# One place among 512 slots for every edge of a graph convolution: one comparison per column, the overflow counts three steps later, the list's chunks two per three steps

## The chip, the cores and the metric

The kernel runs on one core of one Trainium2 chip. The time is that of one execution on the device, in microseconds (us); several runs are given by their median. A core has a TensorE (PE in the profile) for matrix products, a VectorE (DVE), a ScalarE (ACT), a GpSimd (POOL) and a SyncE (SP) that issues transfers. Each works through its own list in order, and they wait for each other by semaphores.

## What is computed

Two relational graph convolutions, a residual and a layer norm, over 1250 nodes of 768 features, 21250 edges and 8 relations:

```python
def _rgcn_conv(x, src, dst, etype, W, root, b):
    x_src = x[src]
    seg = dst * num_rel + etype
    sums = jax.ops.segment_sum(x_src, seg, num_segments=num_nodes * num_rel)
    cnt = jax.ops.segment_sum(jnp.ones((src.shape[0],), dtype=x.dtype), seg, num_segments=num_nodes * num_rel)
    mean = sums / jnp.maximum(cnt, 1.0)[:, None]
    mean = mean.reshape(num_nodes, num_rel, -1)
    out = jnp.einsum('nri,rio->no', mean, W)
    return out + x @ root + b
...
h = jax.nn.relu(_rgcn_conv(x, src, dst, edge_type, W1, root1, b1))
out = _rgcn_conv(h, src, dst, edge_type, W2, root2, b2)
x = _layernorm(x + out)
```

## The kernel before

**The products.** The nodes lie in T = 10 tiles of 125 rows. For one relation the kernel multiplies all node tiles with the relation's weights, in STEPS = 20 steps: a step is one node tile by one half (384) of the output columns. A step is 18 matmuls of 128x384 on PE (L722), because each fp32 product is made of three, high by high, high by low and low by high. ScalarE stages the result (L624), SyncE stores it to `y`. Weights come in half units: a transfer into `w_raw`, ScalarE's `w_high` (L578, released by the steps with s = 1 and s = 11 of each relation), then `w_low`, a subtraction that the GpSimd makes for units 1 to 8 (L463) and the DVE for the others. This text counts steps through the relations: relation 2's s = 1 is step 41, relation 3's s = 11 is step 71. Steps 0 to 79 are the first four relations; the product with root1 (`matrix(ROOT1, ...)`) follows.

**The list of edges.** Rows of `y` are later gathered edge by edge and summed by destination. For that the kernel first sorts the edges into slots: for each pair of relation and destination tile (80 keys) 2 blocks of 128 slots, and further blocks for overflows. While PE multiplies, the DVE works out, for the 21250 edges held as 125 partitions by 170 columns, the key, the rank of an edge within its key (`ranks`, L1166 and L1171), and the rank among the overflows (L1179 to L1196). Both rankings need counts summed over the partitions, which is a small matmul of PE: `sum_rows` (L758) before step 16, and `sum_overs` (L764) before step 41, which waits for the DVE's L1186.

Then the list itself is made by matmuls with one-hot matrices, in CHUNKS = 17 chunks of CJ = 10 columns. For a chunk the DVE makes `key_hot` (L1207), `slot_hot` (L1215), `dst_hot` (L1217) and `keyed` (L1220, L1224). `slot_hot` compares, for each of the ten columns, 512 slots: the first 256 with `rank`, the other 256 with `rank2`, in two instructions. PE's `table_chunk` (L863, L867) multiplies them, 50 small matmuls a chunk, and adds all chunks up in PSUM. The buffers are double: the DVE may begin chunk c when PE has counted chunk c - 2 (`chunk_counted`), and PE waits for chunk c by `hot_ready`.

**The order around the change.** It is written out by hand: `chunks_at(step)` says which chunks PE takes behind a step, one behind every second step from TABLE_AT = 46 on, the last behind step 78. When all are counted, the DVE reads the sums (from L1249 on) and makes the indices by which the GpSimd gathers rows of `y` (L476); the first gathered rows are summed (L749) from the root product's step s = 10 on. PE's `sum_flags` stands behind the root product's s = 1.

Of the kernel before, what the change touches and what calls it, by code (L numbers as in the profile page):

```python
# [8 lines left out]
def rgcn_residual_layernorm(nc, x, src, dst, etype, w_all, b1, b2, out):  # L9
# [18 lines left out]
    N, D = x.shape  # L28
# [3 lines left out]
    P = 128  # L32
    K = D // P
    HALF = D // 2
    T = -(-N // P)
# [11 lines left out]
    MEAN_EDGES = NT * E / N / R  # L47
    FULL = int(MEAN_EDGES // P)
    OVER = 2
    OVER_CAPACITY = OVER * P - P // 2  # L50
    BLOCKS = FULL + OVER
    assert FULL == 2 and R == 8
    DIV_SHIFT = 17
# [16 lines left out]
    CJ = 10  # L70
    CHUNKS = EJ // CJ
    ROOT1 = R // 2
    TABLE_AT = 2 * STEPS + 6
    assert N < 2048 and TABLE_AT + 2 * CHUNKS - 1 <= ROOT1 * STEPS
    MEAN1 = R
    ROOT2 = R + 2
    MEAN2 = Q - 1
# [5 lines left out]
    with ctx:  # L83
# [198 lines left out]

        def chunks_at(step):
            n = step - TABLE_AT
            return [n // 2] if n >= 0 and n % 2 == 0 and n // 2 < CHUNKS else []

        def one_relation(g, r):
            return lambda s: [("sum", g, r, t) for t in range(T) if s == 3 + (STEPS - 4) * t // (T - 1)]
# [37 lines left out]
        def banks(shift, turning=False):  # L326
            return lambda s: 2 + s % 2 if turning and s >= T else (s + shift) % BANKS
# [103 lines left out]
        def _(pool):  # L431
# [11 lines left out]
            pool.memset(eps[:], EPS)  # L443
            pool.iota(column_i[:], [[1, P]], base=0, channel_multiplier=0)
            pool.iota(row_base_i[:].rearrange("p (r t) -> p r t", t=T), [[N, R], [0, T]], base=0, channel_multiplier=0)
            pool.iota(slot_i[:, 0:FULL * P], [[1, FULL * P]], base=0, channel_multiplier=0)
            pool.iota(slot_i[:, FULL * P:SLOTS - P // 2], [[1, OVER_CAPACITY]], base=0, channel_multiplier=0)
            pool.iota(slot_i[:, SLOTS - P // 2:SLOTS], [[1, P // 2]], base=P, channel_multiplier=0)
            link(pool.memset(identity[:], 0.0))
            pool.affine_select(out=identity[:], in_=identity[:], compare_op=ALU.not_equal, fill=1.0, base=0,  # L450
                               pattern=[[-1, P]], channel_multiplier=1)
# [257 lines left out]
        def _(pe):  # L709
# [127 lines left out]
            def staged(yc, turning=False):  # L837

                def free(s):
                    if isinstance(yc, int) and yc == 0 and s < BANKS:  # L840
                        return []
                    return [(y_staged, STEPS * yc + s + 1 - (2 if turning and s >= T else BANKS))]
                return free
# [54 lines left out]
            matrix(0, banks(0), lambda s: staged(0)(s) + ([(h_low_ready, 2 * s + 2)] if s < T else []), turning_x,  # L898
                   middle=(STEPS - 4, sum_rows))
            matrix(1, banks(0), staged(1))  # L900
            matrix(2, banks(0), staged(2), middle=(1, sum_overs), after=table_chunks(2))
            matrix(3, banks(0), staged(3), after=table_chunks(3))

            for s in range(STEPS):
# [27 lines left out]
        def _(dve):  # L932
# [182 lines left out]
            for t in range(4):  # L1115
# [2 lines left out]
            turns_after = iter((1, 2) * T)  # L1118


            tile, dl, src_f, key, row, gid, flag, rank, spos, rank2, src_up, dl_up, etype_f = \
                [edge_f[:, n, :] for n in range(13)]
            ups = edge_f[:, 10:13, :]
            INT = [edge_i[:, n, :] for n in range(4)]
# [68 lines left out]
                ins = dve.scalar_tensor_tensor(ranks[:, c, :], ranks[:, c, :], small[0:EP, 2, c:c + 1],  # L1193
                                               is_over[:, c, :], ALU.add, ALU.mult)
            link(ins)
            sum_ranks(rank2, T)  # L1196
            link(dve.tensor_scalar(flag, flag, -1.0, 1.0, ALU.mult, ALU.add))
            link(dve.scalar_tensor_tensor(spos, rank, float(P - FULL * P), flag, ALU.add, ALU.mult))
            link(dve.tensor_tensor(rank2, rank2, spos, ALU.add))


            dve.wait_ge(transposed, 2 * T)
            for c in range(CHUNKS):
                if c >= 2:
                    dve.wait_ge(chunk_counted, c - 1)
                cut = slice(c * CJ, (c + 1) * CJ)
                ins = dve.tensor_tensor(key_hot[:, c % 2], small_bf[0:EP, 0, :].unsqueeze(1).to_broadcast([EP, CJ, NB]),  # L1207
                                        key_bf[:, cut].unsqueeze(2).to_broadcast([EP, CJ, NB]), ALU.is_equal)
                ins.then_inc(dve_step, 1)
                steps[0] += 1  # L1210
                made = steps[0]
                for j in range(CJ):
                    e = c * CJ + j
                    for part, of in ((slice(0, FULL * P), rank), (slice(FULL * P, SLOTS), rank2)):
                        dve.tensor_scalar(slot_hot[:, c % 2, j, part], slot[0:EP, part], of[:, e:e + 1], None,  # L1215
                                          ALU.is_equal)
                dve.tensor_tensor(dst_hot[:, c % 2], column[0:EP, :].unsqueeze(1).to_broadcast([EP, CJ, P]),  # L1217
                                  dl_bf[:, cut].unsqueeze(2).to_broadcast([EP, CJ, P]), ALU.is_equal)
                values = ups[:, :, cut].rearrange("p n j -> p j n").unsqueeze(2)
                dve.tensor_tensor(keyed[:, c % 2, :, 0:3 * T].rearrange("p j (t n) -> p j t n", n=3),  # L1220
                                  is_over[:, :, cut].rearrange("p t j -> p j t").unsqueeze(3)
                                  .to_broadcast([EP, CJ, T, 3]), values.to_broadcast([EP, CJ, T, 3]), ALU.mult)
                dve.wait_ge(dve_step, made)
                dve.tensor_tensor(keyed[:, c % 2, :, 3 * T:KEYED].rearrange("p j (k n) -> p j k n", n=2),  # L1224
                                  key_hot[:, c % 2].unsqueeze(3).to_broadcast([EP, CJ, NB, 2]),
                                  values[:, :, :, 0:2].to_broadcast([EP, CJ, NB, 2]), ALU.mult)\
                    .then_inc(hot_ready, 1)
# [1 line left out]

            dve.scalar_tensor_tensor(row, etype_f, float(N), src_f, ALU.mult, ALU.add)  # L1230
            dve.scalar_tensor_tensor(gid, key, float(P), dl, ALU.mult, ALU.add)
            link(dve.tensor_scalar(flag, rank2, float(OVER_CAPACITY), None, ALU.is_ge))
            dve.tensor_copy(payload[:, :, 0], row)
            dve.tensor_copy(payload[:, :, 1], gid)
            link(dve.tensor_tensor_scan(spos, flag, flag, 0.0, ALU.add, ALU.max))
# [147 lines left out]
```

## Time and profile before

| | us |
|---|---|
| median of 3 runs | 1595.92 (1595.27 to 1596.81) |
| the profiled execution | 1587.02 |
| its span | 1585.2 |
| PE busy | 1480.5 (93% of the span) |
| DVE busy | 1047.0 (66%) |
| POOL busy | 617.9 (39%) |
| ACT busy | 573.1 (36%) |

The span is the time between the first and the last instruction of the program in the profile. Busy time is the time in which an engine had an instruction under way. PE overlaps its matmuls, so that each row of one is longer than the distance to the next; the DVE's instructions overlap a little too when none waits for the one before it. The granted clock is the share of TensorE's full clock that it was given.

### The profile page before, as it was taken

The numbers are of one execution on the slowest core, as the hardware profiler recorded it, in microseconds if no ns is written. First come the engines' busy times: TensorE is split into PE (matmuls) and PEld (weight loads), VectorE is DVE, ScalarE is ACT, GpSimd is POOL, SyncE is SP. The second block draws the span as 40 slices with busy tenths as digits, with TensorE's granted clock in tenths as the row PEclk, the third lists the DMA queues.
The fourth block names the chain that finished last, engine by engine and source line by source line (L and its number), as shares of the span: only waits on it lengthen the run. The fifth ranks groups of instructions, "written<-read, shape, count | busy, mean of one in ns | idle before, by whom it ended". The sixth has DMA issues, their size and how long they took to land.

```text
span 1585.2 us, 23968 instructions
## 1 busy us (share of the span) xinstructions
PE 1480.5 (93%) x9014; PEld 1458.6 (92%) x9014; DVE 1047.0 (66%) x1767; ACT 573.1 (36%) x818; POOL 617.9 (39%) x456
## 2 busy tenths in 40 slices
PE   5999799999999997998989799999999999899995
PEld 5999689989999997998989799999999999899895
DVE  6899999984877675786971022545454545488697
ACT  3222111111344453485552110333333333358442
POOL 1121111121678784664720320424343434366461
PEclk9999899999999998999999899999999999999998
DMA  5353131232667775775523441646465556577443
GB/s 162 114 187 124 38 99 45 75 97 91 208 210 216 240 243 186 219 223 178 142 83 131 146 158 40 194 154 208 158 200 174 189 177 191 171 235 208 120 143 125
DMA packets 102647, 249.80 MB, mean 158 GB/s; under 512 B 12607, under 2 KB 75758, under 8 KB 102486
## 3 DMA queue, kind: packets, MB, share of 16 engines
q0 software_dynamic: 31680, 131.81, 27.4%
q1 hardware_dynamic: 70870, 116.69, 22.2%
q8 instruction: 62, 1.02, 0.2%
q14 instruction: 35, 0.29, 0.0%
HBM read 204.47 MB, written 65.49 MB: 170 GB/s over the span
## 4 chain that ended last, share of the span: by engine, by line
PE 55%; DVE 22%; DMA 13%; issue 3%; POOL 3%; ACT 2%; SPq 0%; POOLq 0%; DVEq 0%; ACTq 0%
PE prod L722 43%; PE agg L749 11%; DMA raw<-y,bucket_index 6%; DMA y<-y_stage 5%; DVE slot_hot L1215 5%; POOL raw L476 2%; DVE ranks L1171 2%; DVE ranks L1166 2%; DMA x_rows<-in_x 2%; DVE keyed L1224 2%; DVE g_low L988 2%; DVE dst_hot L1217 1%; DVE ranks L1158 1%; DVE g_low L991 1%; PE prod L713 1%
## 5 line engine op out<-in xcount | busy, mean ns | idle before, releaser
L722 PE MATMUL prod<-w_high,h_high 128*128 128x384 f32 x2160 | 735.0, 340 | 20.4 <-ACT y_stage L624 13.3
L722 PE MATMUL prod<-w_low,h_high 128*128 128x384 f32 x2160 | 728.3, 337 | 0.0
L722 PE MATMUL prod<-w_high,h_low 128*128 128x384 f32 x2160 | 727.8, 337 | 0.0
L476 POOL DMA_INDIRECT raw<-y,bucket_index x380 | 494.2, 1301 | 542.3 <-DVE g_low L991 279.3
L991 DVE TENSOR_TENSOR g_low<-raw,g_high 128x768 fp32r<-128x768 f32 x280 | 259.6, 957 | 300.5 <-ACT g_high L591 298.9
L722 PEld LDWEIGHTS prod<-w_high,h_high 128*128 128x128 f32 x2160 | 410.9, 190 | 23.0 <-ACT y_stage L624 15.9
L722 PEld LDWEIGHTS prod<-w_low,h_high 128*128 128x128 f32 x2160 | 410.7, 190 | 0.0
L722 PEld LDWEIGHTS prod<-w_high,h_low 128*128 128x128 f32 x2160 | 409.8, 190 | 0.0
L624 ACT ACTIVATE y_stage<-prod 128x384 f32<-128x384 f32 x280 | 137.5, 492 | 723.5 <-PE prod L722 654.8
L591 ACT ACTIVATE g_high<-raw 128x768 fp32r<-128x768 f32 x300 | 243.2, 842 | 98.1 <-DMA raw<-y,bucket_index 78.5
L749 PE MATMUL agg<-g_high,one_hot 128*128 128x384 f32 x760 | 201.8, 347 | 22.5 <-DVE g_low L991 19.9
L749 PE MATMUL agg<-g_low,one_hot 128*128 128x384 f32 x680 | 175.6, 339 | 0.0
L749 PEld LDWEIGHTS agg<-g_high,one_hot 128*128 128x128 f32 x760 | 135.6, 189 | 33.1 <-issue 21.7
L463 POOL TENSOR_TENSOR w_low<-w_raw,w_high 128x2304 fp32r<-128x2304 f32 x8 | 47.3, 5911 | 266.0 <-ACT w_high L578 266.0
L749 PEld LDWEIGHTS agg<-g_low,one_hot 128*128 128x128 f32 x680 | 125.6, 190 | 0.0
L1001 DVE SCALAR_TENSOR_TENSOR acc<-agg,inv_count,acc 128x768 f32<-128x768 f32 x120 | 121.5, 1012 | 6.0 <-PE agg L749 5.8
L947 DVE TENSOR_TENSOR w_low<-w_raw,w_high 128x2304 fp32r<-128x2304 f32 (+1 forms) x37 | 72.8, 1967 | 56.5 <-ACT w_high L578 56.5
L578 ACT ACTIVATE w_high<-w_raw 128x2304 fp32r<-128x2304 f32 x36 | 76.5, 2126 | 58.0 <-PE prod L722 41.4
L588 ACT ACTIVATE g_high<-raw,scale 128x768 fp32r<-128x768 f32 x80 | 71.2, 932 | 69.7 <-DMA raw<-y,bucket_index 34.5
L980 DVE TENSOR_SCALAR one_hot<-column,dst_local 128x128 fp32r<-128x128 bf16 x380 | 89.6, 295 | 6.9 <-issue 6.4
L969 DVE TENSOR_TENSOR acc<-prod,acc 128x384 f32<-128x384 f32 x60 | 33.1, 555 | 79.6 <-PE prod L722 79.0
L1215 DVE TENSOR_SCALAR slot_hot<-slot,edge_f 125x256 f16<-125x256 f16 x340 | 82.9, 330 | 0.0
(137 smaller groups left out, 777.8 us busy)
## 6 DMA issues: line engine op xcount, KB each, us to landing
y<-y_stage SPq DMA_DIRECT2D x280, 187.5 KB
w_raw<-in_w_all SPq DMA_DIRECT2D x36, 1152.0 KB, 8.7
raw<-y,bucket_index POOLq DMA_INDIRECT x380, 5.3
x_rows<-in_x SPq DMA_DIRECT2D x10, 375.0 KB
y<-in_x SPq DMA_DIRECT2D x1, 3750.0 KB, 14.9
y<-acc SPq DMA_DIRECT2D x10, 375.0 KB
acc<-in_x SPq DMA_DIRECT2D x10, 375.0 KB
out<-acc SPq DMA_DIRECT2D x10, 375.0 KB
```

The source lines that it names most:

```text
L476: pool.indirect_dma_start(raw[:, i % NRAW, :], None, y[0:written * N, :], bass.IndirectOffsetOnAxis(ap=bucket_index[:, at_column:at_column ...
L578: act.activation(w_high[:, h], w_raw[:], ACT.Copy).then_inc(w_high_ready, 1)
L588: act.activation(g_high[:, split_slot(g, i), :], raw[:, slot, :], ACT.Copy, scale=scale[:, i:i + 1])\
L591: act.activation(g_high[:, split_slot(g, i), :], raw[:, slot, :], ACT.Copy).then_inc(high_ready, 1)
L624: act.activation(y_stage[:, s % BANKS, :], prod[:, bank, 0:HALF], ACT.Copy)\
L722: mm = pe.matmul(prod[:, bank, 0:HALF], left[:, k, t * P:(t + 1) * P], right[:, h, k, :], start=(k == 0 and left is h_high and right is w_ ...
L749: mm = pe.matmul(agg[:, par, c, 0:HALF], one_hot[:, par, b, :], part[:, split_slot(g, i), c * HALF:(c + 1) * HALF], start=(b == 0 and part ...
L947: ins = dve.tensor_tensor(w_low[:, h, part], w_raw[:, part], w_high[:, h, part].bitcast(f32), ALU.subtract)
L980: ins = dve.tensor_scalar(one_hot[:, par, b, :], column[:], dst_local[:, bass.ds(column_of(r, t, b), 1)], None, ALU.is_equal)
L991: ins = dve.tensor_tensor(low[p:P, split_slot(g, i), :], rows, high, ALU.subtract)
L1001: ins = dve.scalar_tensor_tensor(a, agg[:, t % 2, :, 0:HALF], inv_count[:, bass.ds(r * T + t, 1)], a, ALU.mult, ALU.add)
L1215: dve.tensor_scalar(slot_hot[:, c % 2, j, part], slot[0:EP, part], of[:, e:e + 1], None, ALU.is_equal)
```

## The change

- The DVE works out one number for each edge, `place`, among all 512 slots: the rank where it is below 256, 256 plus the overflow rank for an overflow, and for relation 0, whose third block is half of the last one, the rank plus 128. `slot` holds 0 to 447 and then 384 to 447. So `slot_hot` is one comparison of 512 columns for each edge column. Ahead of the chunks this takes five small operations in place of three.
- PE's `sum_overs` stands before relation 2's s = 4 (step 44) in place of s = 1 (step 41).
- `chunks_at` gives two chunks per three steps: behind steps 51, 52, 54, 55, 57, 58, ... and the last behind step 75.

```diff
-    TABLE_AT = 2 * STEPS + 6
-    assert N < 2048 and TABLE_AT + 2 * CHUNKS - 1 <= ROOT1 * STEPS
+    TABLE_AT = 2 * STEPS + 10
+    assert N < 2048 and TABLE_AT + CHUNKS * 3 // 2 + 1 <= ROOT1 * STEPS
...
         def chunks_at(step):
             n = step - TABLE_AT
-            return [n // 2] if n >= 0 and n % 2 == 0 and n // 2 < CHUNKS else []
+            return range(n * 2 // 3, min((n + 1) * 2 // 3, CHUNKS)) if n >= 0 else range(0)
...
-            pool.iota(slot_i[:, 0:FULL * P], [[1, FULL * P]], base=0, channel_multiplier=0)
-            pool.iota(slot_i[:, FULL * P:SLOTS - P // 2], [[1, OVER_CAPACITY]], base=0, channel_multiplier=0)
-            pool.iota(slot_i[:, SLOTS - P // 2:SLOTS], [[1, P // 2]], base=P, channel_multiplier=0)
+            pool.iota(slot_i[:, 0:SLOTS - P // 2], [[1, SLOTS - P // 2]], base=0, channel_multiplier=0)
+            pool.iota(slot_i[:, SLOTS - P // 2:SLOTS], [[1, P // 2]], base=SLOTS - P, channel_multiplier=0)
...
-            matrix(2, banks(0), staged(2), middle=(1, sum_overs), after=table_chunks(2))
+            matrix(2, banks(0), staged(2), middle=(4, sum_overs), after=table_chunks(2))
...
-            sum_ranks(rank2, T)
-            link(dve.tensor_scalar(flag, flag, -1.0, 1.0, ALU.mult, ALU.add))
-            link(dve.scalar_tensor_tensor(spos, rank, float(P - FULL * P), flag, ALU.add, ALU.mult))
-            link(dve.tensor_tensor(rank2, rank2, spos, ALU.add))
+            sum_ranks(place, T)
+            dve.tensor_scalar(gid, spos, -1.0, 1.0, ALU.mult, ALU.add)
+            link(dve.scalar_tensor_tensor(row, rank, float(FULL * P), spos, ALU.is_ge, ALU.add))
+            link(dve.tensor_tensor(gid, gid, rank, ALU.mult))
+            link(dve.scalar_tensor_tensor(gid, row, float(P), gid, ALU.mult, ALU.add))
+            link(dve.tensor_tensor(place, place, gid, ALU.add))
...
-                    for part, of in ((slice(0, FULL * P), rank), (slice(FULL * P, SLOTS), rank2)):
-                        dve.tensor_scalar(slot_hot[:, c % 2, j, part], slot[0:EP, part], of[:, e:e + 1], None,
-                                          ALU.is_equal)
+                    dve.tensor_scalar(slot_hot[:, c % 2, j, :], slot[0:EP, :], place[:, e:e + 1], None, ALU.is_equal)
...
-            link(dve.tensor_scalar(flag, rank2, float(OVER_CAPACITY), None, ALU.is_ge))
+            link(dve.tensor_scalar(flag, place, float(SLOTS - P // 2), None, ALU.is_ge))
```

The lines of the changed kernel stand two lower from the DVE's part on, so that L1215 becomes L1214 and L764 becomes L762.

The DVE's instructions ahead of the first chunk and in it, before:

```order
L1161 TENSOR_TENSOR edge_f<-ranks 125x170 [waits dve_step]
L1197 TENSOR_SCALAR edge_f<-edge_f 125x170 [waits dve_step]
L1198 SCALAR_TENSOR_TENSOR edge_f<-edge_f 125x170 [waits dve_step]
L1199 TENSOR_TENSOR edge_f<-edge_f 125x170 [waits dve_step]
L1207 TENSOR_TENSOR key_hot<-small_bf,key_bf 125x800 [waits transposed,dve_step]
L1215 TENSOR_SCALAR slot_hot<-slot,edge_f 125x256 x20
L1217 TENSOR_TENSOR dst_hot<-column,dl_bf 125x1280
L1220 TENSOR_TENSOR keyed<-is_key,edge_f 125x10x30
L1224 TENSOR_TENSOR keyed<-key_hot,edge_f 125x10x160 [waits dve_step]
```

The same place of the changed kernel:

```order
L1159 TENSOR_TENSOR edge_f<-ranks 125x170 [waits dve_step]
L1195 TENSOR_SCALAR edge_f<-edge_f 125x170 [waits dve_step]
L1196 SCALAR_TENSOR_TENSOR edge_f<-edge_f 125x170
L1197 TENSOR_TENSOR edge_f<-edge_f 125x170 [waits dve_step]
L1198 SCALAR_TENSOR_TENSOR edge_f<-edge_f 125x170 [waits dve_step]
L1199 TENSOR_TENSOR edge_f<-edge_f 125x170 [waits dve_step]
L1207 TENSOR_TENSOR key_hot<-small_bf,key_bf 125x800 [waits transposed,dve_step]
L1214 TENSOR_SCALAR slot_hot<-slot,edge_f 125x512 x10
L1215 TENSOR_TENSOR dst_hot<-column,dl_bf 125x1280
L1218 TENSOR_TENSOR keyed<-is_key,edge_f 125x10x30
L1222 TENSOR_TENSOR keyed<-key_hot,edge_f 125x10x160 [waits dve_step]
```

Twenty comparisons of 256 columns have become ten of 512, and two operations of 170 columns have come in ahead of key_hot.

PE from step 50 on, before. Each row that waits for `y_staged` is the first matmul of a step, the seventeen others are left out; each that waits for `hot_ready` is the first of a chunk:

```order
L722 MATMUL prod<-w_high,h_high 128x384 [waits y_staged,w_low_ready,w_high_ready]
...
L863 MATMUL agg<-keyed_60,slot_hot_59 128x160 [waits hot_ready]
...
L722 MATMUL prod<-w_high,h_high 128x384 [waits y_staged]
...
L722 MATMUL prod<-w_high,h_high 128x384 [waits y_staged]
...
L863 MATMUL agg<-keyed_60,slot_hot_59 128x160 [waits hot_ready]
...
L722 MATMUL prod<-w_high,h_high 128x384 [waits y_staged]
```

PE from step 50 on in the changed kernel:

```order
L720 MATMUL prod<-w_high,h_high 128x384 [waits y_staged,w_low_ready,w_high_ready]
...
L720 MATMUL prod<-w_high,h_high 128x384 [waits y_staged]
...
L861 MATMUL agg<-keyed_60,slot_hot_59 128x160 [waits hot_ready]
...
L720 MATMUL prod<-w_high,h_high 128x384 [waits y_staged]
...
L861 MATMUL agg<-keyed_60,slot_hot_59 128x160 [waits hot_ready]
...
L720 MATMUL prod<-w_high,h_high 128x384 [waits y_staged]
```

Chunk 2 stood behind step 50 and chunk 3 behind step 52; now chunk 0 stands behind step 51 and chunk 1 behind step 52.

## Rows read from the trace of the kernel before

**Rows 1.** Waits of PE, whole span: us in total, times, longest us
```profile
PE agg L749 <- DVE g_low L991: 19.9, 10, 8.0
...
PE prod L722 <- ACT y_stage L624: 13.3, 4, 10.0
PE agg L863 <- DVE keyed L1224: 10.7, 4, 3.7
PE agg L764 <- DVE small_bf L1186: 9.6, 1, 9.6
```

**Rows 2.** Chain of work that ended last: start us, us, what
```profile
56.43 24.99 PE prod L722 x144
```

**Rows 3.** Timeline of PE, steps 40 to 79: start, us, instruction [idle before <-releaser]
```profile
159.21 0.34 PE L722 MATMUL prod<-w_high,h_low 128*128 128x384 f32 x1
...
192.90 0.36 PE L863 MATMUL agg<-keyed,slot_hot 125*128 125x160 f16 x4 [2.19 <-DVE keyed L1224]
...
241.95 0.36 PE L863 MATMUL agg<-keyed,slot_hot 125*128 125x160 f16 x4
...
244.20 0.42 PE L722 MATMUL prod<-w_high,h_high 128*128 128x384 f32 x1
...
250.53 0.36 PE L863 MATMUL agg<-keyed,slot_hot 125*128 125x160 f16 x4
...
345.28 0.42 PE L722 MATMUL prod<-w_high,h_high 128*128 128x384 f32 x1
```

**Rows 4.** Stretches: us, busy of PE, PEld, DVE, ACT, POOL, PEclk, DMA share, GB/s
```profile
169.10:174.80 5.70, 5.70 (x19) 5.70 (x20) 5.63 (x9) 0.00 (x0) 0.00 (x0) 0.50 0.00 0
174.80:229.40 54.60, 50.44 (x436) 49.33 (x434) 54.24 (x132) 10.92 (x16) 10.74 (x2) 1.00 0.23 70
...
325.00:328.40 3.40, 3.40 (x42) 3.40 (x40) 3.40 (x18) 0.00 (x0) 0.00 (x0) 0.50 0.71 262
```

**Rows 5.** Timeline of the DVE, start of chunk 0 and chunk 7
```profile
184.40 0.99 DVE L1207 TENSOR_TENSOR key_hot<-small_bf,key_bf 125x800 bf16<-125x800 bf16 x1
...
247.66 0.99 DVE L1207 TENSOR_TENSOR key_hot<-small_bf,key_bf 125x800 bf16<-125x800 bf16 x1
248.56 4.01 DVE L1215 TENSOR_SCALAR slot_hot<-slot,edge_f 125x256 f16<-125x256 f16 x20
...
256.00 1.00 DVE L1207 TENSOR_TENSOR key_hot<-small_bf,key_bf 125x800 bf16<-125x800 bf16 x1
```

**Rows 6.** Lines of the DVE: count, ns min/median/max, first and last start, shapes
```profile
L1215 DVE TENSOR_SCALAR slot_hot<-slot,edge_f x340: 271/286/5242, 185.3 to 337.2; 125x256 f16<-125x256 f16 x170
...
L1232 DVE TENSOR_SCALAR edge_f<-edge_f x1: 249/249/249, 341.4 to 341.4; 125x170 f32<-125x170 f32 x1
...
L1290 DVE TENSOR_SCALAR edge_f<-edge_f,small x1: 309/309/309, 355.8 to 355.8; 125x170 f32<-125x170 f32 x1
...
L1340 DVE TENSOR_SCALAR acc<-acc,moments,std x10: 678/679/681, 1537.4 to 1575.6; 128x768 f32<-128x768 f32 x10
```

**Rows 7.** Timeline of DVE and POOL around a w_low of the GpSimd, chunk 4
```profile
218.67 8.88 DVE L1215 TENSOR_SCALAR slot_hot<-slot,edge_f 125x256 f16<-125x256 f16 x20
...
218.35 5.39 POOL L463 TENSOR_TENSOR w_low<-w_raw,w_high 128x2304 fp32r<-128x2304 f32 x1 [35.28 <-ACT w_high L578]
```

**Rows 8.** Timeline of ACT and POOL behind step 41
```profile
175.13 0.49 ACT L624 ACTIVATE y_stage<-prod 128x384 f32<-128x384 f32 x1 [15.05 <-PE prod L722]
...
177.72 5.35 POOL L463 TENSOR_TENSOR w_low<-w_raw,w_high 128x2304 fp32r<-128x2304 f32 x1 [36.59 <-ACT w_high L578]
```

**Rows 9.** Timeline of DVE and POOL: other meetings, and the counting
```profile
68.79 3.70 DVE L1147 TENSOR_REDUCE small<-is_key 125x20 f32<-125x3400 bf16 x1
72.52 4.26 DVE L1150 CAST small_bf<-small 125x80 bf16<-125x80 f32 x1
...
164.95 1.93 DVE L1183 TENSOR_TENSOR is_key<-over_bf,small_bf 125x1700 bf16<-125x1700 bf16 x1
...
102.89 8.96 POOL L463 TENSOR_TENSOR w_low<-w_raw,w_high 128x2304 fp32r<-128x2304 f32 x1 [26.17 <-ACT w_high L578]
```

More of the change, by code:

```diff
@@ L49, in rgcn_residual_layernorm @@
     OVER = 2
-    OVER_CAPACITY = OVER * P - P // 2
     BLOCKS = FULL + OVER
@@ L1118, in _ @@
             turns_after = iter((1, 2) * T)
-            tile, dl, src_f, key, row, gid, flag, rank, spos, rank2, src_up, dl_up, etype_f = \
+            tile, dl, src_f, key, row, gid, flag, rank, spos, place, src_up, dl_up, etype_f = \
                 [edge_f[:, n, :] for n in range(13)]
```

## The prediction

> **What bounds the kernel now.** By the page TensorE (PE) is busy for 93% of the span, so time is to be had only where PE waits, and the waits come first. Over the whole span they are 86.8 us; 20.3 us belong to the code that is edited: 9.6 us once for the overflow counts (L764 waits for the DVE's L1186), and 10.7 us in four waits for a chunk (L863 waits for L1224), the longest 3.7 [rows 1]. All five lie in the products of steps 41 to 79 (20 steps to a relation, counted through).
>
> Next, what this stretch would take without a wait. 144 matmuls are eight steps and take 24.99 us: 3.12 us a step [rows 2]. A chunk starts at 241.95 us, the product behind it at 244.20, the next chunk after two steps at 250.53 [rows 3]: 2.25 us and 6.33 for two steps, so 2.34 us for a chunk with what it adds to the steps. The last matmul before the long wait ends at 159.55; 39 x 3.12 + 17 x 2.34 = 161.5 us later, at 321.0, step 79 would be over. It begins at 345.28 [rows 3] and so ends at 348.4. **27.4 us are lost.** 20.3 are the waits. The rest is mostly the clock: behind the wait of 9.6 us the granted clock is 0.50 (1.2 GHz) for 5.7 us, behind the last of the four, of 3.5, for 3.4 us; behind the 2.2 us at 192.90 [rows 3] it stays at 1.00 (2.4 GHz) [rows 4]. PE is busy in these stretches and does half, so such a fall costs 1.7 to 2.85 us.
>
> Then the DVE, for which PE waits. It is never idle here. A chunk takes it 8.34 us, from one key_hot (L1207) at 247.66 to the next at 256.00, and 20 comparisons take 4.01 us in all; with 286 ns for the last that is (4.01 - 0.29) / 19 = 196 ns from one to the next, 3.9 us a chunk [rows 5, 6]. PE needs 8.58 us for a chunk and two steps: a slack of 0.24 us. What makes PE wait is the GpSimd. While its w_low subtraction (L463, 5 us) runs, the DVE stands: the 20 comparisons at 218.67 take 8.88 us beside L463 from 218.35 to 223.74 [rows 7]. There are four such meetings behind step 40, released through ScalarE's w_high by the ends of steps 41, 51, 61 and 71, and each of the four chunk waits follows one.
>
> **The comparisons.** 340 of 256 columns become 170 of 512. No row shows 512; the price follows from how such rows grow. An fp32 tensor_scalar of 170 columns with constants lasts 249 ns, and 309 with its scalar read per partition, as here: the scalar costs 60. The fp32 768 columns of L1340 with two such scalars last 679: 679 - 120 - 249 = 310 ns for 598 more columns, 0.52 ns each, which leaves 249 - 88 = 161 fixed. The 16-bit 256 columns last 286: 286 - 161 - 60 = 65 ns, 0.25 each [rows 6]. So 256 more columns add 67 ns, 353 in all, and 196 + 67 = 263 from one to the next. The bounds are 196 (width is free) and 392 (nothing is saved). I take 263, since three shapes agree on the parts. An edge saves 392 - 263 = 129 ns, a chunk 1.3 us: **the DVE needs 7.05 us a chunk**.
>
> The Trainium skill has a rule that speaks against this (VectorE: DVE Perf Modes, "The TRN2 errata"): 58 cycles plus columns over mode. It would make a 256-column comparison 127 ns and a wide one 194, saving 60 ns an edge instead of 129 and, in the walk below, all of the gain. The trace has 196 for the first; the same section adds that its 58 was measured as about 150, which is nearer to the rows.
>
> **The place arithmetic** ahead of chunk 0 grows from three operations of 170 columns to five, of 249 ns to about 340 less the overlap [rows 6]: 0.5 us on the DVE, once. The GpSimd's three iotas become two in the first 3 us, when PE waits for x: nothing. The compare with 448: nothing.
>
> **sum_overs, from ahead of step 41 to ahead of step 44.** The counts were ready at 169.1, PE was there at 159.55. Now PE comes at 168.9, and the wait would be gone. But steps 41 to 43 run early, and so does what they release. Step 41 ended at 175.1 (ScalarE's L624 starts at 175.13) and L463 started at 177.72, 2.6 us behind it [rows 8]. Now it ends at 162.7, and L463 asks at 165.3, amid the counting: L1183 runs 164.95 to 166.88, then the reduction, then the cast L1186. Rows tell what such a meeting does: a running scan is let finish (L463 at 102.89 took 8.96 us: until the scan was done, and 5 more), a reduction that was running kept its 3.70 us, and the cast behind it took 4.26 [rows 9]. So L463 holds from 166.9 to 171.9, the reduction passes beside it, L1186 lands at 172.1, and PE **waits 3.4 us** instead of 9.6. Held too, the reduction would make it 5.3. The DVE loses 3.2 us here instead of 4.9, and starts chunk 0 at 184.4 [rows 5] - 1.6 + 0.5 = 183.3.
>
> **The chunks: after steps 46, 48, ... 78 before, after 51, 52, 54, 55, ... 75 now.** Three steps and two chunks take PE 9.36 + 4.68 = 14.04 us, two chunks take the DVE 14.10: level, with no slack for the meetings behind steps 51, 61 and 71. And with two buffers the DVE may start chunk c only when PE is done with c - 2. I walk both through by these figures, with 4.9 us for a meeting, and 1.8 us of clock for each wait over 3 us (the 1.7 of the wait nearest in length, rounded up). PE goes on at 172.3 + 1.8, ends step 51 at 199.1 and chunk 0 at 201.4. Chunks 0 and 1 have been ready since 190.5 and 197.5, so the DVE stands for 4 us. The meeting behind step 51 falls on chunk 2 (ready at 213.4, PE waits 0.4); chunk 3 costs 1.6, chunks 4 to 7 come within 0.1. The meeting behind step 61 delays chunk 8: 3.4 us and a fall of the clock. 9 to 14 are on time; the meeting behind step 71 delays chunk 15 to 314.9: 4.9 us and a third fall. Chunk 16 is done at 327.6, and four steps later, **at 340.1, step 79 ends**. The same walk with the old figures (46, 48, ..., 196 ns, 9.6 us at step 41) gives chunk waits of 2.7, 3.9, 1.9 and 3.7 us and an end at 348.9; the trace has 2.2, 3.7, 1.3, 3.5 and 348.4.
>
> **Sum.** Lost: 13.7 us of waits and 5.4 of clock, 19.1 instead of 27.4. Gain **8.3 us**. Behind step 79 nothing keeps the old time: the gathers need the end of the chunks (327.6, 345.5 before), the DVE's flags hang on PE's step 81, and stores, weight loads and the remaining waits, for g_low and y_stage [rows 1], on work that PE's steps release. So I move all of the rest by 8.3 us. The profiled execution took 1587.0 us (span 1585.2), the median of the runs is 8.9 more. A wait saved is the same in both: 1595.9 - 8.3 = **1587.6 us**.
>
> **Rivals.** (a) **A smaller fixed share**: about 330 ns from one wide comparison to the next. A chunk is then 7.7 us on the DVE against PE's 7.0, the walk finds ten waits of 0.5 to 6.3 us and ends at 349.5: 1597, no change. Against it stand the three shapes of [rows 6]. The rule of the Trainium skill named above leads here. 10 in 100. (b) **Slower**: width costs in proportion, 392 ns. The denser placing then hurts: DVE 16.7 us for two chunks, PE 14.0, and a later start behind two buffers; the walk ends at 356.4: 1604. It turns to a loss from about 330 ns on. For it: no row of 512. Against: 0.77 ns a column is more than even the fp32 rows have. 7 in 100. (c) **The clock doesn't fall**: 2.2 us left it at 1.00, 3.5 and more did not, and the new waits are 3.4, 3.4 and 4.9. Without falls the walk ends at 336.5: 1584. 20 in 100. (d) **The gain is lost behind**: the waits for y_stage (longest 10.0 us) and g_low [rows 1] grow, because gathers, stores and weight loads meet differently. They keep PE's own pace, so 8 in 100, for 1593 to 1597. (e) The reduction is held as well: the walk ends at 342 to 343, 1590; this belongs to the forecast's own spread.
>
> **How the numbers follow.** Forecast with (e), 1586 to 1591: 55 in 100; (c) 20, (a) 10, (d) 8, (b) 7. The low end, 1582, is (c) with the counts a little sooner. The high end, 1596, takes in most of (d) and a comparison of up to 310 ns; (b) and most of (a) are left out. A measurement of this kernel can tell about 0.2%, 3.2 us, from no change. Faster by more: 0.77 (forecast, (c), a little of (d)). Within: 0.16. Slower: 0.07.
>
> **What the changed profile would show.** slot_hot as one line of 170, 340 to 360 ns each, ten in 2.7 us, and a chunk every 7.05 us. sum_overs waiting 3 to 5.5 us, with an L463 just ahead. PE's longest waits for keyed at chunks 8 and 15, both behind an L463. The last chunk matmul near 327.6 us, ROOT1's first near 340, and from there to the end the length of now. I would be wrong if slot_hot lasted 420 ns or more, if the wait for the counts stayed near 10 us, or if the part behind step 79 changed its length by over 3 us.

## The result, and the profile after

| | before | changed |
|---|---|---|
| median of 13 runs each, us | 1591.0 (1583.2 to 1596.8) | 1576.7 (1572.2 to 1585.5) |
| the profiled execution | 1587.02 | 1582.24 |
| its span | 1585.2 | 1580.4 |
| step 80 begins, in it | 348.5 | 335.6 |
| from there to the end of the span | 1236.7 | 1244.8 |

The ratio is 0.992 [0.9901, 0.994], a gain of 12.7 us of 1591.0 (9.5 to 15.8 by the interval; the two medians differ by 14.3). A second measurement of the same two kernels gave 0.9923 [0.9892, 0.9954]. The time lies 11 us below the forecast of 1587.6 and below the range, which ended at 1582. Two things are mixed in this. The three runs that the sum was set against (1595.92) were the upper end of what the kernel before does; over 13 runs its median is 4.9 us lower. And the gain was sized at 8.3 us. Of the 10.9 us, 4.9 are the first and 6.0 (14.3 - 8.3) the second.

The two profiled executions differ by 4.8 us only. The edited stretch gives 12.9 us, and 8.1 come back behind it. The section on the reasons shows that about half of the 8.1 belongs to this one execution of before.

Waits of PE over the whole span of the changed kernel (us in total, times, longest us), to be read beside [rows 1]:

```profile
PE agg L747 <- DVE g_low L989: 20.6, 10, 4.6
...
PE prod L720 <- ACT y_stage L622: 12.8, 4, 9.8
PE agg L861 <- DVE keyed L1222: 8.2, 4, 4.7
...
PE agg L762 <- DVE small_bf L1184: 3.0, 1, 3.0
```

The wait for the counts went from 9.6 to 3.0 us, the four waits for chunks from 10.7 to 8.2. The two large waits of the later part stay. PE's timeline places three of the waits in the edited stretch, and step 80 behind it:

```profile
171.31 0.19 PE L762 MATMUL agg<-small_bf,before 125*128 125x10 bf16 x1 [3.01 <-DVE small_bf L1184]
...
266.56 0.45 PE L861 MATMUL agg<-keyed,slot_hot 125*128 125x160 f16 x2 [4.75 <-DVE keyed L1222]
...
320.76 0.31 PE L861 MATMUL agg<-keyed,slot_hot 125*128 125x160 f16 x2 [1.74 <-DVE keyed L1222]
...
335.60 0.34 PE L720 MATMUL prod<-w_high,h_high 128*128 128x384 f32 x1
```

Two more, of 0.28 and 1.41 us, stand before chunks 2 and 3. The granted clock, by stretches (us, busy of PE, PEld, DVE, ACT, POOL, PEclk, DMA share, GB/s):

```profile
171.00:174.40 3.40, 3.09 (x11) 3.09 (x12) 3.40 (x2) 0.00 (x0) 0.22 (x1) 0.50 0.05 19
174.40:266.60 92.20, 85.76 (x821) 83.64 (x820) 88.02 (x162) 14.35 (x23) 15.77 (x2) 1.00 0.22 71
266.60:270.00 3.40, 3.40 (x42) 3.40 (x43) 3.40 (x12) 0.00 (x0) 0.00 (x0) 0.50 0.00 0
270.00:335.60 65.60, 63.86 (x631) 62.60 (x629) 57.52 (x124) 8.90 (x15) 18.68 (x7) 1.00 0.31 94
```

The clock falls to 0.50 (1.2 GHz) twice, for 3.4 us each, in which PE is busy for 3.1 and 3.4 us; at half speed that costs 1.6 and 1.7 us. This is behind the wait of 3.01 and the one of 4.75. Behind the one of 1.74 it stays at 1.00.

The DVE's timeline of the changed kernel, with the counting, the place arithmetic up to key_hot's first start at 182.29, and some chunks:

```profile
166.30 1.92 DVE L1183 TENSOR_REDUCE small<-is_key 125x10 f32<-125x1700 bf16 x1
168.26 3.00 DVE L1184 CAST small_bf<-small 125x10 bf16<-125x10 f32 x1
...
180.65 0.25 DVE L1195 TENSOR_SCALAR edge_f<-edge_f 125x170 f32<-125x170 f32 x1
...
182.29 0.99 DVE L1207 TENSOR_TENSOR key_hot<-small_bf,key_bf 125x800 bf16<-125x800 bf16 x1
...
200.28 0.99 DVE L1207 TENSOR_TENSOR key_hot<-small_bf,key_bf 125x800 bf16<-125x800 bf16 x1 [3.80 <-PE agg L865]
201.19 7.57 DVE L1214 TENSOR_SCALAR slot_hot<-slot,edge_f 125x512 f16<-125x512 f16 x10
...
233.34 0.99 DVE L1207 TENSOR_TENSOR key_hot<-small_bf,key_bf 125x800 bf16<-125x800 bf16 x1
234.24 2.71 DVE L1214 TENSOR_SCALAR slot_hot<-slot,edge_f 125x512 f16<-125x512 f16 x10
...
240.39 0.99 DVE L1207 TENSOR_TENSOR key_hot<-small_bf,key_bf 125x800 bf16<-125x800 bf16 x1
...
254.49 0.99 DVE L1207 TENSOR_TENSOR key_hot<-small_bf,key_bf 125x800 bf16<-125x800 bf16 x1
255.39 5.23 DVE L1214 TENSOR_SCALAR slot_hot<-slot,edge_f 125x512 f16<-125x512 f16 x1
```

And the line of the comparisons (count, ns min/median/max, first and last start):

```profile
L1214 DVE TENSOR_SCALAR slot_hot<-slot,edge_f x170: 334/344/5228, 183.2 to 316.8; 125x512 f16<-125x512 f16 x170
```

A wide comparison lasts 344 ns, ten take 2.71 us, so (2.71 - 0.34) / 9 = 0.263 us from one to the next; a chunk takes 240.39 - 233.34 = 7.05 us.

Last, the GpSimd's four w_low subtractions behind step 40:

```profile
164.69 6.53 POOL L461 TENSOR_TENSOR w_low<-w_raw,w_high 128x2304 fp32r<-128x2304 f32 x1 [24.16 <-ACT w_high L576]
...
200.60 5.64 POOL L461 TENSOR_TENSOR w_low<-w_raw,w_high 128x2304 fp32r<-128x2304 f32 x1 [29.38 <-ACT w_high L576]
...
250.33 10.13 POOL L461 TENSOR_TENSOR w_low<-w_raw,w_high 128x2304 fp32r<-128x2304 f32 x1 [44.09 <-ACT w_high L576]
...
304.45 10.22 POOL L461 TENSOR_TENSOR w_low<-w_raw,w_high 128x2304 fp32r<-128x2304 f32 x1 [43.99 <-ACT w_high L576]
```

The last two take 10.1 and 10.2 us in place of 5. The third asks at 250.33, while the DVE works on chunk 8. The DVE goes on undisturbed to 255.39; there its next comparison takes 5.23 us, and both are done by 260.6. Up to 255.39 no comparison is longer than usual, so by this reading the first 5 us of the 10 are not work but the GpSimd standing until the DVE's series lets it in. This is what the prediction did not have.

### The profile page after: what moved, and what is told of

Its sections match the earlier page's. It is cut to its first block, busy times and chain, and to the rows that moved or that the text cites. A ratio compares the mean times of both kernels' runs of the same rounds, so it can differ in the third digit from the quotient of the medians.

```text
span 1580.4 us, 23799 instructions
## 1 busy us (share of the span) xinstructions
PE 1485.0 (94%) x9014; PEld 1462.6 (93%) x9014; DVE 1022.3 (65%) x1599; ACT 572.7 (36%) x818; POOL 629.2 (40%) x455
## 4 chain that ended last, share of the span: by engine, by line
PE 58%; DVE 20%; DMA 12%; POOL 4%; issue 3%; ACT 2%; SPq 0%; DVEq 0%; ACTq 0%; POOLq 0%
PE prod L720 45%; PE agg L747 11%; DMA y<-y_stage 5%; DMA raw<-y,bucket_index 5%; DVE slot_hot L1214 3%; POOL raw L474 2%; DVE ranks L1169 2%; DVE ranks L1164 2%; DVE keyed L1222 2%; POOL scale L482 1%; DVE dst_hot L1215 1%; DVE g_low L989 1%; PE prod L711 1%; DMA x_rows<-in_x 1%; DVE g_low L986 1%
## 5 line engine op out<-in xcount | busy, mean ns | idle before, releaser
L720 PE MATMUL prod<-w_high,h_high 128*128 128x384 f32 x2160 | 736.3, 341 | 20.2 <-ACT y_stage L622 12.8
L461 POOL TENSOR_TENSOR w_low<-w_raw,w_high 128x2304 fp32r<-128x2304 f32 x8 | 58.7, 7341 | 252.4 <-ACT w_high L576 252.4
L586 ACT ACTIVATE g_high<-raw,scale 128x768 fp32r<-128x768 f32 x80 | 70.8, 931 | 72.3 <-issue 39.4
L1214 DVE TENSOR_SCALAR slot_hot<-slot,edge_f 125x512 f16<-125x512 f16 x170 | 60.6, 430 | 0.0
```

What stands on the lines that cost most here:

```text
L586: act.activation(g_high[:, split_slot(g, i), :], raw[:, slot, :], ACT.Copy, scale=scale[:, i:i + 1])\
L720: mm = pe.matmul(prod[:, bank, 0:HALF], left[:, k, t * P:(t + 1) * P], right[:, h, k, :], start=(k == 0 and left is h_high and right is w_ ...
L1214: dve.tensor_scalar(slot_hot[:, c % 2, j, :], slot[0:EP, :], place[:, e:e + 1], None, ALU.is_equal)
```

## The experiments

Kernels are named by their label. Ratios are against the kernel before, timed alternately on the same chip. "Front" is the time at which step 80 begins, "behind" the rest of the span.

**e1_one**: the wide comparison and its place arithmetic alone, in the old order.

```diff
-    TABLE_AT = 2 * STEPS + 10
...
+    TABLE_AT = 2 * STEPS + 6
...
-            return range(n * 2 // 3, min((n + 1) * 2 // 3, CHUNKS)) if n >= 0 else range(0)
+            return [n // 2] if n >= 0 and n % 2 == 0 and n // 2 < CHUNKS else []
...
-            matrix(2, banks(0), staged(2), middle=(4, sum_overs), after=table_chunks(2))
+            matrix(2, banks(0), staged(2), middle=(1, sum_overs), after=table_chunks(2))
```

> The kernel before with the one comparison alone: chunks behind steps 46, 48, ... 78 and sum_overs before step 41 as before. Walk theory (the time of steps 41 to 79 is set by PE and DVE waiting for each other, and each w_low of the GpSimd costs the DVE 4.95 us at the next slot_hot): one wait of 9.6 us for the counts, about 1.5 us at chunk 0 and no other chunk wait, because the DVE needs 7.05 us a chunk against PE's 8.58; step 79 ends 13.7 us earlier than before, time 0.991 of before, as good as the whole change or a little better. Rival, parts that add up (the counts moved give 6.5 us of the change's 12.7): 0.996.

Measured: 1583.45 against 1595.89, 0.9908 [0.9878, 0.9938]; front 334.9. Waits of PE in 158:347:

```profile
PE agg L762 <- DVE small_bf L1184: 9.5, 1, 9.5
PE agg L861 <- DVE keyed L1222: 1.9, 1, 1.9
```

The comparison alone brings all that the whole change brings. The new order, put on top of it, only trades: 9.5 + 1.9 = 11.4 us of waits become 3.0 + 8.2 = 11.2.

**e2_place**: the reverse, the new order alone with the two comparisons of before (the same three places of the code as above, edited in the kernel before).

> The kernel before with the two placements alone (sum_overs before step 44, chunks behind 51, 52, 54, ... 75), with two comparisons of 256. Walk theory: 3 us at the counts, then a wait at nearly every second chunk (1.2 to 7.6 us, about 29 us in all), since the DVE needs 8.34 us a chunk and PE only 7.02; step 79 ends 9 us later than before, time 1.006. Rival, parts that add up: 0.996, faster.

Measured: 1598.84 against 1595.89, 1.0012 [0.9991, 1.0033]; front 356.9. Waits of PE in 158:357:

```profile
PE agg L863 <- DVE keyed L1224: 22.5, 9, 7.3
PE agg L764 <- DVE small_bf L1186: 3.0, 1, 3.0
```

With the old comparison the DVE can't follow two chunks per three steps: nine waits of 22.5 us, where four of 10.7 stood [rows 1], eat more than the 6.6 us that the counts give up. The order gains nothing by itself. Its loss is not measured either: the front is 8.4 us later in the trace, the ratio's interval ends at 1.0033, and the 1.006 that I expected is outside it. This execution's part behind is 1238.0, at the short end of all that were seen (below). The rival, by which the order keeps the 6.6 us of the counts whatever the comparison takes, wanted 0.996, and that is outside too. By the medians the parts multiply: 0.9908 x 1.0012 = 0.992.

**e3_counts**: before with `sum_overs` at step 44 alone.

```diff
-            matrix(2, banks(0), staged(2), middle=(1, sum_overs), after=table_chunks(2))
+            matrix(2, banks(0), staged(2), middle=(4, sum_overs), after=table_chunks(2))
```

> The kernel before with sum_overs before step 44 alone. Walk theory: the wait for the counts falls from 9.6 to 3.0 us, but chunk 0 then waits about 8 us at step 46, since the DVE isn't ready for it sooner; only the DVE's smaller loss to the GpSimd and less lost clock remain: 3.6 us, 0.998. Rival (a wait removed is time gained): 6.5 us of wait and 1 of clock, 0.995.

Measured: 1591.62, 0.997 [0.9947, 0.9993]; front 345.5. Waits of PE in 158:347:

```profile
PE agg L863 <- DVE keyed L1224: 16.5, 4, 7.9
PE agg L764 <- DVE small_bf L1186: 3.0, 1, 3.0
```

and where the longest is (timeline of PE):

```profile
190.11 0.45 PE L863 MATMUL agg<-keyed,slot_hot 125*128 125x160 f16 x2 [7.86 <-DVE keyed L1224]
```

The counts' wait shrinks by 6.6 us, and the one for chunk 0 grows from 2.2 [rows 3] to 7.9: PE comes sooner to a chunk that the DVE finishes at its own pace. Chunk 0 is ready at 190.1 instead of 192.9, since the first w_low now falls on the counting; these 2.8 us are what is left. The ratio's interval holds both the 0.998 that I expected and the 0.995 of the rival, by which a wait removed is time gained; it is the wait of 7.9 in the trace that speaks against the rival.

**e7_counts45**: the changed kernel with `sum_overs` one step later, `middle=(5, sum_overs)`.

> The changed kernel with sum_overs before step 45 instead of 44. Walk theory: PE comes to it at 171.4 us, when the counts are ready, so no wait and no fall of the clock; of the 4.7 us won, 0.8 go to a longer wait at chunk 2; step 79 ends 3.9 us earlier than in the changed kernel, time 0.990 of before. Rival (chunk waits take all of it back, as they did where the counts alone were moved): as the changed kernel.

Measured: 1580.55 against 1592.28, 0.9893 [0.985, 0.9935]; front 332.7. Waits of PE in 158:347:

```profile
PE agg L861 <- DVE keyed L1222: 8.2, 4, 4.7
```

The wait for the counts is gone with its clock fall, and the chunk waits don't grow in sum (0.3 at chunk 2 became 0.9, 1.7 at chunk 16 became 1.1). 335.6 - 332.7 = 2.9 us in the trace of the 3.0 + 1.6 that stood there: in this execution step 40 ended 0.9 us later, and the fall behind the wait of 4.75 lasted 5.0 us. The timed intervals of the two kernels overlap.

**e8_no_meeting**: before, but from relation 2's second half on the DVE itself makes w_low, in place of the GpSimd.

```diff
-    NEAR = 9
+    NEAR = 6
...
             for c in range(CHUNKS):
+                if c in (5, 10, 15):
+                    low_of_unit(5 + c // 5)
                 if c >= 2:
                     dve.wait_ge(chunk_counted, c - 1)
```

> The kernel before, with the w_low of units 6, 7 and 8 made by the DVE ahead of chunks 5, 10 and 15 instead of by the GpSimd; two comparisons and the old placement. Theory M (the GpSimd's subtraction stops the DVE for 4.95 us each time, and that is what makes PE wait for chunks): the DVE pays 2.55 us for each instead of 4.95, the chunk waits of 3.7, 1.3 and 3.5 us become three of about 1.3 without a fall of the clock; step 79 ends 9.3 us earlier than before, 0.994. Rival (the DVE is simply too slow for a chunk, the meetings are beside the point): the DVE has more work than before, so slower, 1.003.

Measured: 1584.17 against 1592.28, 0.9937 [0.9911, 0.9963]; front 339.0. Waits of PE in 158:347, and the subtraction on the DVE's timeline:

```profile
PE agg L764 <- DVE small_bf L1186: 9.5, 1, 9.5
PE agg L863 <- DVE keyed L1226: 4.4, 3, 2.6
```

```profile
225.60 2.55 DVE L947 TENSOR_TENSOR w_low<-w_raw,w_high 128x2304 fp32r<-128x2304 f32 x1
```

The DVE does in 2.55 us of its own time what the GpSimd did at a price of 4.9 us of the DVE's. Three such exchanges take 6.3 us off the chunk waits (10.7 to 4.4) and 9.5 off the front, part of it in falls of the clock (three in this stretch before, two here). So the meetings were most of the chunk waits of before. The wait that stays, 2.6 us before chunk 0, stands ahead of all three exchanges.

**e9_gap**: before, with the wait for key_hot moved from ahead of the last keyed to ahead of the comparisons, so that the DVE's series has another place to pause.

```diff
-                made = steps[0]
+                dve.wait_ge(dve_step, steps[0])
...
-                dve.wait_ge(dve_step, made)
```

> The kernel before, with the DVE's wait for its own key_hot moved ahead of the 20 comparisons of each chunk (before, it stood ahead of the last operation, where it cost nothing). So the DVE stands still once a chunk until key_hot has landed. Theory K (in the second profile of the kernel before, one L463 lasted 44.4 us and PE then waited 12.8 us at step 70, because the DVE's instructions, back to back, kept the GpSimd out): every L463 now gets in within a chunk's 8.4 us, so none is over 14 us and PE never waits at steps 70 or 80; the DVE pays about 0.1 us a chunk; median 0.998 to 1.001 of before, and no run as slow as the slowest of before. Rival (the 44.4 us came from elsewhere, as from memory or the weights' transfer): no difference of that kind, about 1.001.

Measured: 1596.22 against 1595.24, 1.0011 [0.9987, 1.0035]; front 348.7. All four subtractions took 5.2 to 5.8 us. So they did in two of the three profiled executions of the unchanged kernel. The median lies at the top of the 0.998 to 1.001 that I expected, and the rival's 1.001 is as near; this run tells nothing apart. What decides at which instruction the GpSimd gets in stays open.

**e5_before, e11_before, e6_after**: the two kernels unchanged, profiled again (e6_after also timed), to see what varies from execution to execution.

> The kernel before, unchanged, for a second profile. Theory V (what differs behind step 79 in single profiled executions is variation of one execution from another, not the change): steps 41 to 79 as in the first profile, step 79 over near 348.4 us, but the part behind step 79, 1236.7 us in the first profile, is longer here, 1238 to 1250. Rival S (the change makes that part longer): again 1236 to 1238.

> The kernel before, unchanged, for a third profile. Theory K: it shows either L463 of 5 to 10 us each and step 79 over near 348 us, or again one of tens of us with a wait of PE at step 70 or 80 behind it; and the part behind step 79 lies between 1236 and 1250 us. Rival S (behind step 79 the kernel before always needs 1236 to 1238 us): 1236 to 1238.

> The changed kernel, unchanged, for a second profile and in a session with the next two. Waits of 3.0, 0.3, 1.4, 4.8 and 1.7 us again in steps 41 to 79 and step 79 over near 335.5. Theory V: the part behind differs from its 1244.8 us by several us, ratio 0.991 to 0.993. Rival S: 1244 to 1246.

Measured: e5_before span 1598.2, front 357.5, behind 1240.7. e11_before span 1592.8, front 346.9, behind 1245.9. e6_after span 1582.6, front 337.1, behind 1245.5; 1582.5 against 1592.28 in medians. The expectation that the part behind would differ from the first profile's by several us failed for e6_after (1245.5 and 1244.8), and the rival by which the kernel before always has a short one failed with e11_before. In e5_before something else was seen, on the timelines of POOL and of PE:

```profile
267.32 44.42 POOL L463 TENSOR_TENSOR w_low<-w_raw,w_high 128x2304 fp32r<-128x2304 f32 x1 [41.72 <-ACT w_high L578]
```

```profile
311.85 0.66 PE L722 MATMUL prod<-w_high,h_high 128*128 128x384 f32 x1 [12.77 <-issue]
```

A subtraction of 5 us took 44.4: the DVE ran chunk after chunk, each comparison at its usual length, and the GpSimd was held out until PE itself, at step 70, needed that w_low. PE stood 12.8 us, and the DVE stopped at 306.8 for lack of a counted chunk, after which the subtraction ended. This execution lost some 9 us of front by it (357.5 against 348.5); I take it for the same behaviour as the 10 us subtractions above, carried further; that it ended 4.9 us after the DVE had stopped fits this.

**e4_fit**: the changed kernel with each chunk behind the step by which the DVE has it ready, and the counts at step 45.

```diff
-    TABLE_AT = 2 * STEPS + 10
...
+    AFTER = (51, 52, 55, 57, 58, 60, 61, 63, 66, 67, 69, 70, 72, 73, 76, 78, 79)
...
-            n = step - TABLE_AT
-            return range(n * 2 // 3, min((n + 1) * 2 // 3, CHUNKS)) if n >= 0 else range(0)
+            return [c for c in range(CHUNKS) if AFTER[c] == step]
...
-            matrix(2, banks(0), staged(2), middle=(4, sum_overs), after=table_chunks(2))
+            matrix(2, banks(0), staged(2), middle=(5, sum_overs), after=table_chunks(2))
```

> The changed kernel with sum_overs before step 45 and the chunks behind steps 51, 52, 55, 57, 58, 60, 61, 63, 66, 67, 69, 70, 72, 73, 76, 78, 79, placed where the walk has the DVE ready, the meetings with the GpSimd counted in. Walk theory: no wait over 0.5 us from step 41 to 79 and no fall of the clock there, step 79 ends at 320.4 us of the span, 27 us earlier than before and 15 earlier than the changed kernel: 0.983 of before. Rival L (gains in front are lost behind, in the gathers, since the profiled execution of the changed kernel kept only 4.8 of 12.9 us): no more than 0.990.

Measured: 1567.63 against 1595.89, 0.9819 [0.9787, 0.9851], clearly ahead of both kernels. PE has no wait between 159.9 and 321.7; the stretch:

```profile
159.90:321.70 161.80, 161.80 (x1554) 158.84 (x1553) 158.96 (x278) 29.31 (x45) 31.02 (x4) 1.00 0.25 78
```

The granted clock is 1.00 throughout. 161.65 us from the end of step 40 (160.07, where ScalarE stages it) to step 80 (321.72) are the 161.5 that the prediction had worked out for a stretch without waits. Against the kernel before that is a gain of 26.8 us in the trace (348.5 - 321.7) and of 28.9 +/- 5 in the runs.

**e10_fit_low**: e4_fit, and the DVE makes three of the four w_low as in e8_no_meeting, ahead of chunks 3, 9 and 15.

> The kernel of e4_fit with the w_low of units 6, 7 and 8 made by the DVE ahead of chunks 3, 9 and 15. Walk theory: steps 41 to 79 had no wait left in e4_fit, so the DVE's 7 us more of slack are worth nothing: the same time as e4_fit, 0.982 of before, step 79 over near 321. Rival (what still varies in e4_fit is the GpSimd's meetings): 2 us or more faster.

Measured: 1569.62 against 1595.24, 0.9858 [0.9829, 0.9886]; front 321.2. Where PE no longer waits, 7 us less of the DVE's time (152.1 us busy in place of 159.0, of 162) are worth nothing; the median is even 2 us above e4_fit's, with overlapping intervals, and the 0.982 that I expected lies just outside.

## Why the prediction was wrong in size and right in kind

**The level.** The sum was moved onto the median of three runs, 1595.9. With the 13 runs it would have stood at 1591.0 - 8.3 = 1582.7. 4.9 of the 10.9 us of error are this. The range took nothing in for it. Of the other 6.0, the edited stretch explains 12.9 - 8.3 = 4.6 in the traces, and 1.4 is less than the ratio's interval can tell.

**The comparison: right.** 353 ns long and 263 from one to the next were forecast, 344 and 263 measured; 7.05 us a chunk forecast and measured. The breakdown of [rows 6] (fixed part, per-partition scalar, columns) held for a width of which no row existed. The rival of 330 ns and that of 392 are out. So is the rule of the Trainium skill (VectorE: DVE Perf Modes, "The TRN2 errata"): it gave 60 ns saved for an edge column, the rows give 392 - 263 = 129.

**The place arithmetic: right.** 180.65 to 182.29, 1.64 us for five operations, against 249 ns and two of 340 before.

**The counts: right.** 3.4 forecast, 3.0 measured. The meeting fell where it was put: L461 enters at 166.3 beside the reduction, which keeps its 1.92 us, and the cast behind it takes 3.00. The Trainium skill (SBUF — State Buffer, "Who interferes with whom") has the DVE and the GpSimd exclude each other on a shared pair of ports, and excepts reductions on trn2; the trace agrees.

**The chunks: the failed step.** The walk let the GpSimd's subtraction in at the moment at which it asked, "the meeting behind step 61 delays chunk 8", "the meeting behind step 71 delays chunk 15". In the trace it asks during chunks 8 and 15 and gets in one chunk later, at the first comparison behind the next key_hot (255.39 and 309.62). The delays fall on chunks 9 and 16:

| | forecast | measured |
|---|---|---|
| counts | 3.4 | 3.0 |
| chunks 2 and 3 | 0.4 + 1.6 | 0.3 + 1.4 |
| behind step 61 | 3.4 (chunk 8) | 4.75 (chunk 9) |
| behind step 71 | 4.9 (chunk 15) | 1.74 (chunk 16) |
| clock | 3 falls of 1.8 | 2 falls, of 1.6 and 1.7 |
| lost in all | 19.1 | 14.5 by these terms |

Behind step 71 it matters most. Chunk 15 stands one step behind chunk 14, chunk 16 two steps behind chunk 15, so PE comes to chunk 16 with a step more behind it: of the 4.9 us it met 1.74, and with a wait so short the third fall of the clock didn't come. That is 3.2 + 1.8 of the difference. Chunk 9 is the other way round, one step behind chunk 8, and there 1.35 go back. As a whole: ScalarE stages step 40 at 158.98 in the changed kernel (159.59 before), and 335.60 - 158.95 - 161.5 = 15.2 us were lost up to step 80, where before it was 27.4. The gain of the stretch is therefore 12.2 us in this pair instead of 8.3. The remaining 0.6 of the 12.9 is step 40's earlier end. It looks like variation from execution to execution: the w_low subtraction that starts at 70.95 in the changed kernel and at 71.56 in the one before starts from 70.8 to 72.1 in the thirteen profiled executions, and the kernels with the wide comparison (70.95 to 72.04) and those without it (70.81 to 72.14) overlap wholly.

The same walk, started from this trace (step 40 over at 158.95, chunk 0 begun at 182.29) and with the one rule changed, so that the GpSimd gets in at the next first comparison of a chunk, with a meeting of 4.95 us (a comparison of 5228 ns less 0.263) and 1.7 us of clock behind waits of 2.9 and more, ends at 335.8; the trace has 335.6. The rule was made after the fact, on this trace. It holds for all 12 meetings with chunks in the four profiled executions of the changed kernel, e7_counts45 and e4_fit, and e4_fit, placed by it, has no wait left. It is no law. In e1_one the three subtractions get in at a key_hot. And in the kernel before, chunk 9, the GpSimd is let in at once in the middle of the series, at the twelfth comparison:

```profile
264.33 1.00 DVE L1207 TENSOR_TENSOR key_hot<-small_bf,key_bf 125x800 bf16<-125x800 bf16 x1
265.24 7.40 DVE L1215 TENSOR_SCALAR slot_hot<-slot,edge_f 125x256 f16<-125x256 f16 x12
...
267.38 5.17 POOL L463 TENSOR_TENSOR w_low<-w_raw,w_high 128x2304 fp32r<-128x2304 f32 x1 [43.64 <-ACT w_high L578]
```

Over all executions, a GpSimd that asks among comparisons of 256 columns is let in within 0.2 us in 8 cases of 9; the ninth is the one held out for 39 us (e5_before). One that asks among comparisons of 512, with another behind, is let in there in none of 5. So the prediction's picture, in at the moment of asking, was read from a trace in which it held, and with the wide comparison it held no longer. Why the width should matter no run shows.

**"The rest moves by 8.3 us": not decided.** Behind step 80 the first pair of profiles differs by 8.1 us, and over 3 was the prediction's own sign of being wrong. By stretches, before and changed (columns as above):

```profile
348.50:915.80 567.30, 529.21 (x3003) 519.08 (x3003) 357.70 (x573) 247.64 (x340) 307.21 (x240) 0.98 0.57 180
915.80:1585.20 669.40, 641.17 (x3662) 635.47 (x3660) 368.06 (x577) 258.48 (x369) 257.68 (x191) 0.98 0.53 167
```

```profile
335.60:911.40 575.80, 537.77 (x3003) 526.50 (x3003) 353.79 (x563) 247.53 (x340) 302.10 (x234) 0.96 0.56 176
911.40:1580.40 669.00, 640.61 (x3662) 635.58 (x3660) 368.43 (x577) 258.15 (x369) 257.25 (x191) 0.98 0.53 167
```

The last 669 us are the same. The 8.5 us lie in steps 80 to 199, at a granted clock of 0.96 instead of 0.98. Profiled again, the kernel before has 570.6 and 576.9 us there, the changed one 577.3: the first profile of before was the shortest of three. Of the whole part behind, before has 1236.7, 1240.7 and 1245.9 us (mean 1241.1), the changed kernel 1244.8 and 1245.5: about 4 of the 8.1 us belong to that one execution, and 4 are left, less than the three of before differ among themselves. Thirteen profiled executions of ten kernels have 567 to 583 us in this stretch and 667 to 673 in the last one. The four longest (578.8 to 582.6) belong to kernels whose front ends by 335, the two with the latest fronts (357 and more) have 569.0 and 570.6. So a lengthening by a few us behind an earlier front is not excluded; the other runs, 567.3 to 577.3 at fronts of 336 to 349, show no order. This stays open. The timed gains against the gains in the front (348.5 less the front) don't settle it: 12.7 and 12.9 us for the changed kernel, 28.9 and 26.8 for e4_fit, 14.7 and 13.6 for e1_one, 17.0 and 15.8 for e7_counts45, but 22.7 and 27.3 for e10_fit_low, and e2_place, whose front is 8.4 later, lost 1.9 (at most 5.3).

**The clock rival.** "Without falls" is out: both waits of 3 us and more were followed by one. But the bound between 2.2 and 3.5 us that the prediction read from four waits is no bound. Over all profiled executions, of the waits of PE in this stretch that are 2.0 us or shorter (16, from 0.9 on) none was followed by a fall; of those of 2.15 to 2.9 us (13) ten were, 2.15 among them, and 2.19, 2.51 and 2.54 were not; of those of 3.0 and more (22) all but one, of 3.45. The prediction also passed over a fall in its own trace: behind the wait of 3.7 us the clock was at 0.50 as well, for 5.1 us, 2.6 us lost, and with it the 27.4 are complete (20.3 + 2.85 + 2.6 + 1.7). And a fall is not of one length: behind the same 3.01 us it lasted 3 us in one execution of the changed kernel and 6 in the other.

## What to carry to other kernels

Where two engines exclude each other, ask not only how long the meeting is but where the one that waits is let in: behind a series without pauses it can be several us later, and the consumer that is hit is another one. A fixed schedule that hands work between two engines is worth fitting to the producer's measured times before, and after, either of them is made faster; here the faster comparison gave 0.9%, the new order that came with it nothing, and placing the same chunks by their finishing times, with the counts one step later, another 1.0% (11.0 of the 13.9 us of front are the chunks, 332.7 - 321.7). And set a forecast against as many runs as there are: a median of three was 0.3% off, 40% of the gain that was to be foretold.

## What the runs showed of the hardware

- A GpSimd tensor_tensor of 2304 fp32 columns, 5.2 us when it gets in at once, stops the DVE's comparisons, casts and two-input operations for 4.9 us, not a reduction. The waiting one has no turn while the DVE's instructions follow each other: 10.1 and 10.2 us in the changed kernel, 44.4 in one execution of before. Not always: among comparisons of 256 columns it was let in within 0.2 us in 8 cases of 9, among those of 512 in none of 5. The same section of the Trainium skill has whoever issues first keep the ports for its whole instruction; the meetings agree. Who comes next when both have asked it leaves open, and there the traces show the DVE ahead, for up to 39 us.
- A 16-bit comparison with its scalar read per partition: 344 ns at 512 columns and 286 at 256, 263 and 196 from one to the next.
- The DVE's own w_low of 2304 columns takes 2.55 us, half of the GpSimd's, and a quarter of what the GpSimd's takes from both engines together (5.2 and 4.9).
- The granted clock isn't set by a wait's length alone: 10 of 13 waits of 2.15 to 2.9 us were followed by 0.50 (1.2 GHz), one of 3.45 was not. A term for it in a sum needs its own range of 0 to 3 us a wait.
